# An attention gather queue with half the clearing between gathers and a count of half steps to wait for

## The reference, cut to what matters

```python
h = (x_flat @ W_gat).reshape(M, HEADS, NUM_EXPERTS)
e = leaky_relu(a_src[src] + a_dst[dst], negative_slope=0.2)
ee = exp(e - segment_max(e, dst)[dst])
alpha = ee / (segment_sum(ee, dst)[dst] + 1e-16)
agg = segment_sum(h[src] * alpha[:, :, None], dst) + b_gat
scores = layernorm(agg).mean(1)                  # top 2 of 4 experts, softmax
for ei in range(NUM_EXPERTS):                    # experts' part needs x only
    hh = gelu(x @ W1[ei] + b1[ei])
    out = out + g[..., None] * (hh @ W2[ei] + b2[ei])
```

## Time and profile before

| | |
|---|---|
| median of 3 runs | 8722.8 us |
| profiled execution, its time | 8751.12 us |
| its span, first to last instruction | 8749.3 us |
| mean granted TensorE clock, of full speed | 0.786 |
| busy in the span: PE, DVE, ACT, POOL | 66%, 51%, 43%, 61% |
| POOL busy with the gathers of L1956 (1122) | 1081.7 us |
| POOL busy with the clearings of L1960 (1122) | 369.4 us |
| first and last gather of the stage start at | 6793.0 and 8429.4 us |

### The profile page before, as it was taken

The page is one execution under the profiler, slowest core; times in us unless marked ns, Lnnn a source line. Parts: engine busy times, 40 slices in busy tenths (PEclk is TensorE's granted clock), DMA queues, the critical chain, the costliest instruction groups (busy, mean ns, idle before and its releaser), DMA issues. The chain is left out here.

```text
span 8749.3 us, 89830 instructions
## 1 busy us (share of the span) xinstructions
PE 5794.4 (66%) x19687; PEld 3832.1 (44%) x19687; DVE 4492.0 (51%) x8804; ACT 3779.5 (43%) x9645; POOL 5355.2 (61%) x5884
## 2 busy tenths in 40 slices
PE   5555555555556999966455555555556988889956
PEld 4333333333345666633343333333333554455634
DVE  5355454555466999956444444444457222222336
ACT  5455565555553222235455555545555222122213
POOL 4666666666644222245666666666656888888871
PEclk8677666776666999988677666766777999999978
DMA  5333333333332111145333233223324322222227
GB/s 150 99 103 98 101 101 101 101 88 90 91 114 71 53 44 49 44 111 182 88 88 90 85 88 88 83 85 87 90 77 153 70 56 50 50 57 55 67 79 271
DMA packets 500460, 797.46 MB, mean 91 GB/s; under 512 B 123070, under 2 KB 365355, under 8 KB 499851
## 3 DMA queue, kind: packets, MB, share of 16 engines
q0 software_dynamic: 200256, 453.47, 19.1%
q1 hardware_dynamic: 299696, 338.23, 12.0%
HBM read 595.60 MB, written 197.30 MB: 91 GB/s over the span
## 5 line engine op out<-in xcount | busy, mean ns | idle before, releaser
L1017 PE MATMUL part<-rows,spread 128*128 x6656 | 2459.9, 525 | 2112.5 <-issue 1060.2
L1017 PEld LDWEIGHTS part<-rows,spread 128*128 128x128 f32 x6656 | 1625.6, 262 | 2891.9 <-issue 2618.4
L974 DVE TENSOR_TENSOR agg<-agg,part 128x257 f32 (+1 forms) x3328 | 1405.2, 422 | 2368.6 <-issue 893.9
L957 POOL DMA_INDIRECT rows<-h,row x1563 | 1544.9, 988 | 867.6 <-issue 443.8
L957 POOL DMA_INDIRECT rows<-f,row x1563 | 1544.2, 988 | 765.3 <-issue 447.2
L1041 ACT ACTIVATE spread<-iota,place 128x128 f32<-128x128 f32 x3328 | 1016.0, 387 | 2149.1 <-PE part L1017 1001.9
L1956 POOL DMA_INDIRECT rows<-gat,src x1122 | 1081.7, 964 | 188.7 <-issue 184.8
L1047 ACT ACTIVATE spread<-spread,weight 128x128 f32<-128x128 f32 x3328 | 1017.5, 388 | 14.5 <-ACT spread L1043 0.8
L2034 PE MATMUL y_ps<-agg,hid 128*128 128x256 f32 x3136 | 806.8, 401 | 146.3 <-issue 134.8
L2034 PEld LDWEIGHTS y_ps<-agg,hid 128*128 128x128 f32 x3136 | 609.4, 198 | 367.1 <-issue 282.3
L2023 PE MATMUL hid_ps<-agg,w 128*128 128x512 f32 (+1 forms) x1600 | 699.8, 589 | 20.4 <-DMA b<-in_L_ffn_b 11.4
(11 more groups left out here) (398 smaller groups left out, 6076.0 us busy)
## 6 DMA issues: line engine op xcount, KB each, us to landing
expert_rows<-y_all SPq DMA_DIRECT2D x196, 256.0 KB
made<-expert_rows SPq DMA_DIRECT2D x49, 1024.0 KB
x<-x SPq DMA_DIRECT2D x42, 896.0 KB
rows<-f,row POOLq DMA_INDIRECT x1563
rows<-h,row POOLq DMA_INDIRECT x1563
rows<-gat,src POOLq DMA_INDIRECT x1122
xbuf<-zero SPq DMA_DIRECT2D x128, 128.0 KB
x<-xbuf SPq DMA_DIRECT2D x32, 512.0 KB
```

The costliest lines, as they stand in the source:

```text
L957: pool.indirect_dma_start(out=rows[:, u, 0:D], out_offset=None, in_=table, in_offset=bass.IndirectOffsetOnAxis(ap=q.row[:, i:i + 1], axis= ...
L974: nc.vector.tensor_tensor(sum_t, sum_t, part[:, p % NB, 0:WIDE], ALU.add).then_inc(added, 1)
L1017: nc.tensor.matmul(part[:, p % NB, 0:WIDE], spread[:, p % (2 * BANKS), :], row_p, start=True, stop=True).then_inc(multiplied, 1)
```

## The change

Two edits in `attend`. The tile `rest` has 128 columns in place of 256, so each of the 1122 clearings writes half as much. And every third gather, from number 54 on (counted from 0 over the whole stage), waits on `y_taken`: gather i waits until 196*i/1122 - 8 half steps (rounded down) have been taken. That is 356 waits, the first for 1 half step and the last, at gather 1119, for 187. A gather stream that reaches 8 half steps of lead so has to hold.

```diff
@@ -1897,6 +1897,7 @@
     wide = lambda n: 2 * P * len(pairs_of(n))
     due = lambda b: HALVES * (b + 1) // GBLOCKS + 1
+    AHEAD, LEAD = 3, 8
@@ -1911,7 +1912,7 @@
-        begun, rest = s.sb("begun", [P, GROWS], F32), s.sb("rest", [P, 2 * P], F32)
+        begun, rest = s.sb("begun", [P, GROWS], F32), s.sb("rest", [P, P], F32)
@@ -1953,6 +1954,8 @@
                     if b >= 3:
                         pool.wait_ge(freed, b - 2)
                     for j in range(B):
+                        if (b * B + j) % AHEAD == 0 and HALVES * (b * B + j) // GREC > LEAD:
+                            pool.wait_ge(y_taken, HALVES * (b * B + j) // GREC - LEAD)
                         pool.indirect_dma_start(out=rows[b % 3][:, j, :], out_offset=None, in_=table,
```

## The result

The changed kernel took 8756.68 us (median of 5 runs, 8735.25 to 8772.04), the kernel before 8718.51 (median of 5). The ratio is 1.0048, with a 95% interval of 1.0032 to 1.0063: some 38 us slower, where 97 us less was forecast, and outside the forecast's range. The profiled execution had a span of 8760.6 us; in it the stage began 30 us earlier than in the profile of before (first gather at 6763.4, not 6793.0), for reasons in earlier stages that the change doesn't touch, so stages are compared, not spans.

A forecast was written before the change was run, and what follows sets the result against it. GpSimd's gather stream was taken to bound the stage, TensorE 22 us behind. Stretches of 371 + 288 + 885 = 1544 us meant 97 us less: 8722.8 - 97 = 8626 us, range 8597 to 8742.

The forecast's parts named there:

- What bounds, and what the clearing saves: GpSimd's gather stream has no slack, TensorE 22 us behind; the shorter clearing saves 107 ns each, 120 us over 1122.
- The waits cost nothing when met: The 356 added waits before gathers: nothing when already met, 36 us as upper bound.
- The price of a gather for TensorE: In slow spells each gather costs TensorE 0.409 us, so a half step takes 9.93 us at a 1.334 us period.
- The three stretches: Takes: 48 half steps bound by gathers, 371 us; 29 with slow TensorE, 288 us; the other 119, 885 us.
- A hold clears the lag: When GpSimd's gathers hold at a wait, TensorE's lag clears, as at the one 3.91 us hold before.
- it keeps TensorE quick: Behind the first hold the old course continues: 7.25 us a half step, 863 us, plus 22 us for slow spells.
- the relapse rival: Lag returns within a few half steps of a hold: rest at 8.06 us a half step, 8699 us; chance 0.18.
- The slower rival: TensorE late all along: 0.409 us a gather everywhere beyond the second stretch, 9.23 us a half step, 8839 us; chance 0.13.
- The sign it gave: Forecast wrong if takes beyond the first hold average over 8.25 us, or GpSimd waits over 100 us in total.
- The clock: TensorE's half-speed clock in the slow stretch: at most 12% of 634 us, costing at most 38 of 180 us missing.
- The sentence of the Trainium skill: Says PE and ACT never wait on anyone; the forecast held the trace disagreed, else GpSimd alone would bound the kernel.
- a TensorE that isn't slowed at all: The rival "POOL alone": gathers set the pace throughout, 120 us less, 8603 us; chance 0.17.

The follow-up runs named there:

- c256_wait: The kernel before plus only the 356 waits, clearing still 256 columns: 8768.63 us, ratio 1.0000 to the kernel before.
- c128_lead2: The changed kernel with a lead of 2 half steps in place of 8: 8807.49 us, ratio 1.0042 to the kernel before.
- start256: The changed kernel with 256 columns cleared behind the first 54 gathers and 128 behind the rest: 8826.76 us, ratio 1.0050 to the kernel before.
- c128_nowait: The kernel before with only the clearing shortened to 128 columns, no added waits: 9183.64 us, ratio 1.0467.
- nogather: The kernel before with gathers and clearings of blocks 3 to 32 left out: 8490.57 us in one run, takes 1347 us.
- busy: As the kernel before, but four chained 256-column clearings replace each gather and clearing in blocks 3 to 32: 8724.67 us in one run, takes 1348 us.
- c60x2: The kernel before with two chained clearings of 60 columns in place of one of 256: 8748.21 us, ratio 1.0038.
- c320_nowait: The kernel before with a clearing of 320 columns, no added waits: 8831.63 us, ratio 1.0061.

## Why the prediction was wrong

**What bounds, and what the clearing saves: right.** GpSimd's stream had no slack, TensorE 22 us behind it, 107 ns a clearing (106 measured), 120 us off GpSimd.

**The waits cost nothing when met: right** (c256_wait, 1.0000).

**The price of a gather for TensorE: wrong, and this is the step that failed.** From the slow stretch before I took 0.409 us a gather and kept it while the period fell from 1.441 to 1.334 us. I counted it in full only until the first hold; in the first stretch it stood at nothing, because I held that to be bound by gathers, and behind the first hold it counted only in slow spells as rare as before. I gave the clearing and the waits bounds, but none to this price. The runs without waits put the excess of their takes over 1347 us at (1781 - 1347)/1122 = 0.39 us a gather at 1.391 us, 0.62 at 1.335 and 0.77 at 1.258; before it was (1611 - 1347)/1122 = 0.24, VectorE's waits for gathers included, and at 1.465 us TensorE idled for takes alone. The clearing that nothing reads was what kept it low. At its worst TensorE issues one product a gather.

**The three stretches.** For the first 48 half steps I had gathers as the limit and 371 us; they took 459 (first gather to 48th take at 7222.1), and TensorE was the limit from the third on. The next 29 took 256 us against 288. The other 119 took 965 us, 8.1 each, against 885. That is 88 us more, 32 less and 80 more; the sum is 1680 and not 1544. The middle term came near by luck: the lead came to 8 half steps not behind the 77th take but behind the 4th, 93 us after the first gather, since TensorE stood still. The kernel before took 387, 282 and 948 us for the same half steps, so the changed one lost 72 us in the first 48. Yet c128_lead2 and start256 show that this is not to be had by a better start alone.

**A hold clears the lag: right; it keeps TensorE quick: wrong.** I read 7.25 us a half step off the stretch behind the one hold of before. The lag, from the start of a half step's last product to its take, was indeed shorter, 2.2 us in the median against 8.3 before. But it kept coming back (under 1 us at the 13th to 15th take, 6.7 and 14.7 at the 16th and 17th), and a short lag is not a quick TensorE. I had taken the loss for PE, ACT and DVE waiting on each other; in the slow stretch before TensorE's second layer waited 1.6 us for takes and 84.6 for nothing that shows. The rest came out as the relapse rival had it, 8.1 us a half step against its 8.06. What put the kernel above that rival's 8699 us is its first stretch, which it still had bound by gathers. The slower rival's mechanism (a gather costs 0.409 us everywhere, 9.23 us a half step) did not hold either: the rest ran at 8.1 to 8.4. The sign it gave did: over 8.25 us a half step behind the first hold, here 8.38, and over 100 us of waits, here 127.7.

**The clock: its share grew.** From 6890 to 8390 the granted clock was 0.93 on average, so at most 14% of the 1500 us ran at 1.2 GHz, which costs at most 105 us, of the 1500 - 179 x 6.885 = 268 us that are missing. In the slow stretch before it was at most 38 of 180 us. Beside unheld gathers (c128_nowait, 8000 to 8500) the clock was 0.83, and 1.00 in nogather. The clock is not the first cause, since it fell only once the products came 1.40 us apart, but it makes the gathers dearer.

**The sentence of the Trainium skill.** "PE and ACT never wait on anyone" (SBUF — State Buffer, Who interferes with whom). That section is on the ports of SBUF, and no run here shows TensorE waiting at one; I read it more widely. As far as clearings go the runs agree even so: 6.8 to 6.9 us a half step beside a GpSimd that clears without a pause (busy). For gathers 1.44 us apart and closer the wide reading doesn't hold for TensorE's issue: 6.8 us without them, 8.4 with them held, 10.4 unheld. The chances I gave lay wrong for the same reason: 0.17 went to a TensorE that isn't slowed at all.

What stays open: through what a gather instruction holds TensorE's issue. It is not the clearing, not GpSimd's semaphores, and mostly not the rows moved. No run told the generation of the gather's descriptors from its transfers in HBM or on the queue, and none whether it was the spacing or the stop at every block that kept TensorE free at 1.465 us. No version was found that beats the kernel before; the nearest is that kernel with the waits added, at 1.0000.

## What to carry to other kernels

A useless instruction in a queue may be there for another engine: before it is shortened, look at who shares the time with the transfers that it keeps apart, and give its effect on them a bound of its own. Where gathers like these run beside dense products, try a spacing first: here 1.465 us left TensorE alone throughout, 1.441 for the first 200 us only, and the price was that the gathers then bound the stage. If they must come closer, let them go one to three at a time against the consumer's progress; long unheld runs cost most. And a price read in one regime (0.41 us a gather at a period of 1.44) is not to be carried to another that no row shows.

## What the runs showed of the hardware

- An indirect gather on GpSimd slows TensorE's issue: with gathers 1.338 us apart and unheld, one product of 256 columns every 1.40 us, where one every 0.22 us is possible. On average 0.28 to 0.30 us of TensorE a gather when a wait stands before every third. Beside gathers 1.465 and 1.499 us apart TensorE had no such idle time (c60x2, c320_nowait).
- It is not the load of the DMA engines: in the standstill they were busy for a tenth of the time and moved 13 GB/s.
- The granted clock was 1.00 before the standstill and 0.57 in it, where TensorE was busy 31.57 of 71 us and had begun to idle first; 1.00 throughout 7000 to 8000 without gathers (nogather).
- A gather for 16 partitions takes 0.86 us on GpSimd, one for 128 takes 0.95 (medians), and the smaller one slows TensorE nearly as much (one run, 1.032 against an estimated 1.044 at the same period).
- A clearing by GpSimd of 128 partitions takes 126, 219, 273 and 325 ns (medians) for 16, 128, 192 and 256 float32 columns, and does nothing to TensorE.
- The standstill moves: avoided at the start (start256), it came behind it, and the ratio was 1.0050 in place of 1.0048.
